# The first loads issued in stages, the experts' weights last, and new numbers in the planner of the order

## The chip, the core and the metric
The kernel runs on one NeuronCore of a Trainium2 chip. Five engines work side by side, each through its own list of instructions in its written order: TensorE (PE) multiplies, and its loads of the stationary operand are shown as PEld; VectorE (DVE); ScalarE (ACT); GpSimd (POOL); SyncE (SP), which here only starts transfers. The engines wait for each other by semaphores. Transfers between the chip's memory and the on-chip buffer (SBUF) are done by 16 DMA engines; nearly all of them are started by SP. Matrix products land in PSUM, which has 8 banks.

The metric is the time of one execution on the device in microseconds, as the median of several. The runs of the kernel before took 1142.59, 1146.7 and 1146.88 us, so the median is 1146.7 us.

## What is computed
Two layers of a Perceiver block for 64 samples of 32 tokens with width 128, everything in float32. Each layer is cross-attention to a context of 257 tokens, self-attention over the 32 tokens, and a mixture of 8 experts of which each token uses two. In outline:

```python
x = x + L0_xattn(layernorm(x), ctx, ctx, mask)   # 16 heads of 8, the mask hides keys
x = x + L0_attn(layernorm(x))                    # causal, with Pluecker lines as an added bias
x = x + L0_ffn(layernorm(x))                     # 8 experts, silu(gate) * up, best 2 of the best 2 groups
x = x + L1_xattn(layernorm(x), ctx, ctx)         # no mask
x = x + L1_attn(layernorm(x))                    # causal
x = x + L1_ffn(layernorm(x))                     # 8 experts, relu, best 2 of 8
return x
# scores of L0_xattn: s = q.k / sqrt(8);  s = s + where(mask == 0, -1e9, s);  softmax over 257 keys
```

## The kernel before
**Tiling.** Four samples make a group of 128 token rows, so there are 16 groups. They are shared out over three streams, 0, 1 and 2, each with its own set of buffers (`ctxT0`, `maskb0`, `P0` and so on). Stream 0 has six turns, streams 1 and 2 have five. The three streams are in flight together, so that PE has work from one while another waits.

**Order.** No engine's order is written by hand. `group_tasks` lists the tasks of one group with their needs: `kproj`, `vproj` and `kvtail` (keys and values from the context), `mask`, `ln`, `lnT`, `qproj`, `bq` (the queries spread out by head, `spread`), `scores`, `soft` (softmax), `ptrans` and `pv` (weights transposed, times values), `tailV`, `sel`, `rT`, `norm`, `oproj` (the end of the cross-attention, in `On` and then `xs`), then `qk`, `vself`, `lines` to `jlines`, `sscore` to `spv` (self-attention), `route` to `pick`, `up` and `down` (the experts). `list_schedule` then plays all tasks of all groups through against a duration for each, and writes down an order for PE, DVE, ACT and POOL, a PSUM bank for each result, and the order of SP's later loads. Which ready task goes first is set by a priority that holds the tables `BONUS` and `WHEN` and the constants `STICK`, `EAGER`, `REACH`, `LAG`. Two more tables tell the planner when inputs come: `FIRST` gives the earliest start of the first tasks of each stream, and `ARRIVES` the delay that it reckons for a reload in later turns (6.0 us for the mask). The tables decide only the order; on the chip each engine waits for what is really there.

**First loads.** SP starts all first loads in one go, without a wait: `bcol` and the first three weights of `wsq`, then for each stream `ctxT` (514 KB), `xin` (64 KB) and four copies of the mask (128.5 KB each), with the constants `cst` in stream 0's part and the other small weights (`wsq`, `brow`, `router`, `b2`) in stream 2's part, and right behind them the experts' weights: `w13` 2048 KB, `w2a` 1024 KB, `w1` 2048 KB, `w2b` 2048 KB. Only then come the reloads of later turns, each of which waits until its buffer is free. The first of them is the mask of stream 0 for its second turn: it waits for the last masked softmax step of stream 0 in the first turn.

**The mask.** A mask is converted on POOL (L718), reduced on DVE (L1152, L1154), and then used by DVE's masked softmax step (L1187). POOL and DVE have the conversion of stream 0's second mask in the middle of their orders, while streams 1 and 2 are still in their first turn: whatever stands behind it on these two engines waits for the transfer too.

**Lines that the prediction speaks of** (of the kernel before; those behind SP's block are 11 higher in the changed kernel): L661, L667, L673 (SP: `ctxT`, `xin`, `maskb`), L688 (SP: experts), L718, L745, L772, L782, L795 and L798, L802 (POOL: mask, `spread`, a square root of the lines, `LQ`, the sums of `norm`, the self-attention's weights), L725 (POOL: `rstd`), L878 (PE: `ptrans`), L913 (PE: `oproj`), L957 (PE: `sscore`), L991 (PE: `up`), L1230 (DVE: `xs` after `oproj`).

Of the kernel before, what the change touches and what calls it, by code (L numbers as in the profile page):

```python
# [399 lines left out]
BONUS = {("bo", 0, PE): -24.56, ("bo", 0, DVE): -172.31, ("bq", 0, POOL): 435.89, ("bq", 1, POOL): 294.24,  # L400
         ("down", 0, PE): -3.88, ("down", 0, DVE): 1140.48, ("down", 1, PE): -23.73, ("down", 1, DVE): -642.6,
         ("groups", 0, DVE): -666.24, ("jlines", 0, PE): 226.43, ("jlines", 0, VACT): -301.7,
         ("kproj", 0, PE): -82.44, ("kproj", 0, VACT): -62.34, ("kproj", 1, PE): -300.02,
         ("kproj", 1, VACT): -421.52, ("kvtail", 0, PE): 65.43, ("kvtail", 0, DVE): -32.49,
         ("kvtail", 1, PE): -706.66, ("kvtail", 1, DVE): -892.6, ("lines", 0, PE): 573.82,
         ("lines", 0, VACT): -1047.17, ("lines", 0, POOL): -14.44, ("linesN", 0, DVE): 410.16,
         ("linesN", 0, POOL): -1284.74, ("linesT", 0, PE): 27.38, ("linesT", 0, VACT): 541.34,
         ("linesT", 0, POOL): 659.68, ("linesU", 0, DVE): 840.54, ("linesU", 0, POOL): 213.22,
         ("ln", 0, DVE): -26.08, ("ln", 0, POOL): 294.5, ("ln", 1, DVE): 13.88, ("ln", 1, POOL): -759.28,
         ("lnT", 0, PE): 445.73, ("lnT", 0, DVE): 687.26, ("lnT", 0, VACT): -105.05, ("lnT", 1, PE): 89.47,  # L410
         ("lnT", 1, DVE): 330.28, ("lnT", 1, VACT): -15.37, ("mask", 0, DVE): -305.15, ("mask", 0, POOL): 38.85,
         ("norm", 0, DVE): 860.3, ("norm", 0, POOL): 92.47, ("norm", 1, DVE): 975.38, ("norm", 1, POOL): 1244.98,
         ("oproj", 0, PE): 567.81, ("oproj", 0, DVE): -251.96, ("oproj", 1, PE): 549.66, ("oproj", 1, DVE): 786.95,
         ("pick", 0, DVE): 450.3, ("pick", 1, DVE): 268.79, ("ptrans", 0, PE): -10.71, ("ptrans", 0, VACT): -29.09,
         ("ptrans", 1, PE): 155.2, ("ptrans", 1, VACT): 530.74, ("pv", 0, PE): 745.89, ("pv", 1, PE): 39.36,
         ("qk", 0, PE): 276.11, ("qk", 0, VACT): 179.08, ("qk", 0, POOL): 1160.11, ("qk", 1, PE): 551.51,
         ("qk", 1, VACT): -30.44, ("qk", 1, POOL): 1198.39, ("qproj", 0, PE): 85.23, ("qproj", 0, VACT): -628.38,
         ("qproj", 1, PE): 386.09, ("qproj", 1, VACT): -252.75, ("rT", 0, PE): -300.59, ("rT", 1, PE): 577.99,
         ("route", 0, PE): 309.97, ("route", 0, DVE): 952.83, ("route", 0, VACT): 1317.83, ("route", 1, PE): 1275.74,
         ("route", 1, DVE): 1019.06, ("route", 1, VACT): -928.27, ("scores", 0, PE): 36.22, ("scores", 1, PE): 32.03,  # L420
# [1012 lines left out]
```

## Time and profile before

| what | value |
|---|---|
| median of three runs | 1146.7 us (1142.59 to 1146.88) |
| the profiled execution's own time | 1144.7 us |
| its span | 1142.9 us |
| mean granted clock of TensorE | 0.988 of full speed |
| PE busy | 1083.9 us, 95% |
| PE weight loads busy | 908.6 us, 80% |
| DVE busy | 838.9 us, 73% |
| ACT busy | 725.8 us, 64% |
| POOL busy | 511.4 us, 45% |
| moved by DMA | 30.33 MB, of it 27.05 MB read from memory |

The span is from the first to the last instruction of one profiled execution. A busy time is the time in which an engine had an instruction in work. PE is busy in 95% of the span, so what can be won without taking work away is the remaining 59.0 us, and what is lost while PE is busy at the lower of its two clocks. The stream of the DMA is dense in the first 44 us only.

### The profile page before, as it was taken

To read this page: it belongs to the slowest core of one execution; us is meant where nothing else is said; L and a number is where in the kernel's file an instruction comes from. 1 tells how busy PE (TensorE), PEld (TensorE's weight loads), DVE (VectorE), ACT (ScalarE), POOL (GpSimd) and SP (SyncE) were. 2 spreads that over 40 slices of the span, in tenths; PEclk is the share of its full clock that TensorE was granted. 3 is DMA by queue.
4 is the path that set the end of the run, shared out by engine and by line. 5 is a ranking of instruction groups with operands and counts; after the bars stand their busy time and mean duration, and the time that the engine had idled before them with its cause. 6 is when DMAs were issued, how large, how long until landed. Compare 5 with 4: busy or idle time off the path is not lost.

```text
span 1142.9 us, 34921 instructions
## 1 busy us (share of the span) xinstructions
PE 1083.9 (95%) x13032; PEld 908.6 (80%) x13032; DVE 838.9 (73%) x2865; ACT 725.8 (64%) x2305; POOL 511.4 (45%) x712
## 2 busy tenths in 40 slices
PE   7798899999999999999999999999999999999898
PEld 5477787788877978887878878788788788887698
DVE  4455977687878866867868688686878757877785
ACT  6682478765676495667575775747657766556742
POOL 5386234435654345355444445354453354343430
PEclk9897999999999999999999999999999999999999
DMA  9520000000010000010000001010000000000000
GB/s 291 193 60 18 2 2 2 25 17 15 20 57 2 5 23 6 21 41 23 22 5 20 5 23 41 13 31 4 23 2 22 2 5 2 5 1 2 2 2 8
DMA packets 17748, 30.33 MB, mean 27 GB/s; under 512 B 2216, under 2 KB 14640, under 8 KB 16944
## 3 DMA queue, kind: packets, MB, share of 16 engines
q1 hardware_dynamic: 15280, 27.06, 7.8%
q8 instruction: 108, 1.77, 0.6%
q10 hardware_dynamic: 2304, 1.05, 0.3%
q14 instruction: 56, 0.46, 0.1%
HBM read 27.05 MB, written 1.05 MB: 25 GB/s over the span
## 4 chain that ended last, share of the span: by engine, by line
PE 61%; DVE 20%; ACT 9%; issue 5%; POOL 4%; DMA 2%; SPq 0%; DVEq 0%; ACTq 0%; POOLq 0%
PE bank L999 12%; PE bank L991 11%; PE bank L878 7%; PE bank L871 5%; PE bank L890 4%; PE bank L845 3%; PE bank L838 3%; PE bank L957 3%; ACT P L1039 3%; PE bank L976 2%; ACT PT L1050 2%; DVE P L1329 2%; DVE P L1319 2%; DMA maskb<-mask_in 2%; DVE xs L1339 2%
## 5 line engine op out<-in xcount | busy, mean ns | idle before, releaser
L991 PE MATMUL bank<-xnT,w 128*128 128x128 f32 x2048 | 259.4, 279 | 5.1 <-DVE P L1322 2.6
L991 PEld LDWEIGHTS bank<-xnT,w 128*128 128x128 f32 x2048 | 242.1, 193 | 11.7 <-issue 3.8
L1050 ACT COPY PT<-bank 128x512 f32<-128x512 f32 x256 | 149.9, 592 | 30.9 <-PE bank L878 29.1
L878 PE MATMUL bank<-cst,P 128*128 128x128 f32 x1024 | 153.8, 279 | 10.7 <-DVE nmax L1187 8.4
L878 PEld LDWEIGHTS bank<-cst,P 128*128 128x128 f32 x1024 | 114.3, 142 | 34.6 <-issue 14.5
L1042 ACT ACTIVATE P<-bank,nmax 128x257 f32<-128x257 f32 x256 | 123.2, 491 | 27.5 <-DVE nmax L1191 26.8
L1039 ACT ACTIVATE P<-P,nmax 128x257 f32<-128x257 f32 x256 | 131.7, 517 | 13.7 <-DVE nmax L1187 13.1
L999 PE MATMUL bank<-w2b,P 128*128 128x128 f32 x1024 | 130.8, 278 | 0.0
L1187 DVE CUSTOM_DVE_ANT_0 P<-bank,maskb,mscale 128x257 f32<-128x257 f32 x256 | 114.0, 481 | 20.9 <-PE bank L871 20.6
L999 PEld LDWEIGHTS bank<-w2b,P 128*128 128x128 f32 x1024 | 121.0, 192 | 5.7 <-issue 4.5
L1191 DVE TENSOR_REDUCE nmax<-bank 128x1 f32<-128x257 f32 x256 | 96.5, 413 | 39.1 <-PE bank L871 38.8
L1339 DVE SCALAR_TENSOR_TENSOR xs<-bank,comb,xs 128x128 f32<-128x128 f32 x256 | 88.2, 345 | 45.0 <-PE bank L999 39.1
L795 POOL TENSOR_TENSOR On<-On 128x256 f32<-128x256 f32 x64 | 46.8, 732 | 140.6 <-DVE On L1223 140.3
L1104 ACT ACTIVATE P<-bank,bcol 128x128 f32<-128x128 f32 x256 | 73.2, 369 | 48.8 <-PE bank L991 35.6
L871 PE MATMUL bank<-KT,spread 32*128 32x257 f32 x1024 | 92.0, 429 | 8.0 <-ACT PT L1050 1.9
L1097 ACT ACTIVATE P<-bank 128x256 f32<-128x256 f32 x128 | 49.4, 388 | 68.2 <-PE bank L991 48.0
L745 POOL TENSOR_TENSOR spread<-qs,cst 128x512 f32<-128x512 f32 x64 | 66.6, 1043 | 55.5 <-ACT qs L1033 32.2
L890 PE MATMUL bank<-PT,V 128*32 128x128 f32 x2048 | 81.9, 280 | 1.5 <-ACT PT L1050 1.5
L999 PE MATMUL bank<-w2a,P 128*128 128x128 f32 x512 | 73.3, 280 | 2.7 <-DVE P L1322 1.9
L838 PE MATMUL bank<-ctxT,wsq 128*128 128x512 f32 x128 | 68.7, 629 | 7.1 <-DMA ctxT<-ctx_in 5.7
L1329 DVE TENSOR_SCALAR P<-bank,bcol 128x128 f32<-128x128 f32 x256 | 71.2, 341 | 5.0 <-PE bank L999 3.1
L890 PEld LDWEIGHTS bank<-PT,V 128*32 128x32 f32 x2048 | 48.8, 109 | 29.1 <-ACT PT L1050 13.6
(133 smaller groups left out, 2198.4 us busy)
## 6 DMA issues: line engine op xcount, KB each, us to landing
ctxT<-ctx_in SPq DMA_DIRECT2D x16, 514.0 KB, 3.7
maskb<-mask_in SPq DMA_DIRECT2D x64, 128.5 KB, 2.8
w<-w_in SPq DMA_DIRECT2D x2, 2048.0 KB, 17.9
w2b<-w2b_in SPq DMA_DIRECT2D x1, 2048.0 KB, 26.1
wsq<-wsq_in SPq DMA_DIRECT2D x1, 1032.0 KB
xin<-x_in SPq DMA_DIRECT2D x16, 64.0 KB, 1.9
w2a<-w2a_in SPq DMA_DIRECT2D x1, 1024.0 KB, 17.2
out<-xs ACTq DMA_DIRECT2D x16, 64.0 KB, 1.5
```

The source lines that it names most:

```text
L838: nc.tensor.matmul(ps[:, :], w(f"k{l}"), ctxT[s][:, m * 512:m * 512 + 512], start=True, stop=True).then_inc(full, 1)
L871: nc.tensor.matmul(bank[bank_of[step, i, g]][:, 0:SK], BQ[s][rows, m, :, :], KT[s][rows, m, :], start=True, stop=True, tile_position=(32 * ...
L878: ins = nc.tensor.transpose(ps[:, k * 128:k * 128 + 128], P[s][:, 2 * m + k // 2, (k % 2) * 128:(k % 2) * 128 + 128], ident)
L890: ins = nc.tensor.matmul(ps[32 * g:32 * g + 32, 128 * m:128 * m + 128], V[s][:, 2 * m + k, 32 * g:32 * g + 32], PT[:, place_of[s, l, m, i] ...
L991: ins = nc.tensor.matmul(ps[:, k * 128:k * 128 + 128], wt[:, m, k * 128:k * 128 + 128], xnT[s][:, :], start=True, stop=True)
L999: ins = nc.tensor.matmul(ps[:, 0:128], HT[s][m % SLOTS][:, k * 128:k * 128 + 128], wt[:, m, k, :], start=(k == 0), stop=(k == nk - 1))
L1039: nc.scalar.activation(P[s][:, m, :], P[s][:, m, :], ACT.Exp, bias=nmax[s][:, m:m + 1], scale=-1.0, accum_out=sums[s][:, m:m + 1]).then_in ...
L1042: nc.scalar.activation(P[s][:, m, :], ps[:, 0:SK], ACT.Exp, bias=nmax[s][:, m:m + 1], accum_out=sums[s][:, m:m + 1]).then_inc(exp_done[s], 1)
L1050: nc.scalar.copy(PT[:, place, m % 2 * 512:m % 2 * 512 + 512], ps[:, :]).then_inc(pt_done[s], 1)
L1187: nc.vector.tensor_tensor_reduce(P[s][:, m, :], ps[:, 0:SK], mbias[s][:, b, :], mscale[s][:, b:b + 1], LOWEST, ALU.add, ALU.min, nmax[s][: ...
L1191: nc.vector.tensor_reduce(nmax[s][:, m:m + 1], ps[:, 0:SK], X, ALU.max, negate=True).then_inc(max_done[s], 1)
L1339: nc.vector.scalar_tensor_tensor(xs[s][:, :], ps[:, 0:128], comb[s][:, m:m + 1], xs[s][:, :], ALU.mult, ALU.add).then_inc(x_done[s], 1)
```

## The change
SP's first loads are the same transfers of the same sizes. They are now issued in stages, and SP waits between them: after `ctxT0`, `xin0` and `cst` it waits for `ctxT0` to land; then come the mask of stream 0, `ctxT1`, `xin1`; a wait for that mask; the mask of stream 1, `ctxT2`, `xin2`; a wait for `ctxT1`; the other small weights; a wait for the mask of stream 1; the mask of stream 2; a wait for the small weights; `w13` and `w2a`; a wait for these two; `w1` and `w2b`. The reloads of the second turn follow as before. The planner's `FIRST` has new numbers, and `STICK`, `EAGER`, `LAG`, `BONUS` and `WHEN` have new ones too, so the order of all four computing engines changes from the first turn to the last. Tasks, durations in the planner, tiles and instructions are the same.

```diff
@@ -100,8 +100,8 @@
-FIRST = {("kproj", PE): (4.8, 9.7, 13.6), ("ln", DVE): (5.2, 10.0, 13.9), ("xpb", POOL): (5.2, 10.0, 13.9),
-         ("mask", POOL): (7.9, 11.8, 19.5), ("bo", PE): (20.5,), ("up", PE): (30.0, 30.0, 30.0)}
+FIRST = {("kproj", PE): (5.8, 9.5, 13.0), ("ln", DVE): (5.8, 9.5, 13.0), ("xpb", POOL): (5.8, 9.5, 13.0),
+         ("mask", POOL): (9.5, 13.0, 20.0), ("bo", PE): (18.0,), ("up", PE): (32.0, 32.0, 32.0)}
@@ -395,47 +395,47 @@
-STICK = 0.421
-EAGER, REACH, LAG = 0.1333, 0.001, 32.81
-BONUS = {("bo", 0, PE): -24.56, ("bo", 0, DVE): -172.31, ("bq", 0, POOL): 435.89, ("bq", 1, POOL): 294.24,
...
+STICK = 0.690
+EAGER, REACH, LAG = 0.0412, 0.000, 30.07
+BONUS = {("bo", 0, PE): -482.13, ("bo", 0, DVE): -413.15, ("bq", 0, POOL): 535.15, ("bq", 1, POOL): 113.54,
...
@@ -673,19 +673,30 @@
-            for s in range(STREAMS):
-                load_ctx(0, s)
-                load_x(0, s)
-                if s == 0:
-                    sp.dma_start(cst[:, :], const_d).then_inc(constants_in, 16)
-                elif s == STREAMS - 1:
-                    for dst, src in ((wsq[:, WFIRST:WSQ], wsq_d[:, WFIRST:WSQ]), (rows_in, brow_d[:, 0:512]),
-                                     (router[:, :], brow_d[:, 512:520]), (b2[:, :], b2_d)):
-                        sp.dma_start(dst, src).then_inc(others_in, 16)
-                load_mask(0, s)
-            for dst, src, loaded in ((w13[:, :, :], w13_d, experts0_in), (w2a[:, :, :, :], w2a_d, experts0_in),
-                                     (w1[:, :, :], w1_d, experts1_in), (w2b[:, :, :, :], w2b_d, experts1_in)):
-                sp.dma_start(dst, src).then_inc(loaded, 16)
+            load_ctx(0, 0)
+            load_x(0, 0)
+            sp.dma_start(cst[:, :], const_d).then_inc(constants_in, 16)
+
+            sp.wait_ge(ctx_in[0], 16)
+            load_mask(0, 0)
+            load_ctx(0, 1)
+            load_x(0, 1)
+            sp.wait_ge(mask_in[0], 64)
+            load_mask(0, 1)
+            load_ctx(0, 2)
+            load_x(0, 2)
+            sp.wait_ge(ctx_in[1], 16)
+            for dst, src in ((wsq[:, WFIRST:WSQ], wsq_d[:, WFIRST:WSQ]), (rows_in, brow_d[:, 0:512]),
+                             (router[:, :], brow_d[:, 512:520]), (b2[:, :], b2_d)):
+                sp.dma_start(dst, src).then_inc(others_in, 16)
+            sp.wait_ge(mask_in[1], 64)
+            load_mask(0, 2)
+            sp.wait_ge(others_in, 16 * OTHER_LOADS)
+            for dst, src in ((w13[:, :, :], w13_d), (w2a[:, :, :, :], w2a_d)):
+                sp.dma_start(dst, src).then_inc(experts0_in, 16)
+            sp.wait_ge(experts0_in, 16 * EXPERT_LOADS)
+            for dst, src in ((w1[:, :, :], w1_d), (w2b[:, :, :, :], w2b_d)):
+                sp.dma_start(dst, src).then_inc(experts1_in, 16)
```

Two places of the new order matter below. The first is DVE around the second mask of stream 0. `mmin0` and `mscale0` are the two steps on that mask, `P1,nmax1` is one masked softmax step of stream 1, `On0` the end of stream 0's cross-attention in the first turn and `xs0` its result. Before:

```order
L1187 ISA P1,nmax1<-bank4,maskb1,mscale1 128x257
L1187 ISA nmax1 128x1
L1209 TENSOR_TENSOR On0<-bank1,On0 128x4x4x32
L1152 TENSOR_REDUCE mmin0<-maskb0 128x4
L1154 TENSOR_SCALAR mscale0<-mmin0 128x4
L1187 ISA P1,nmax1<-bank4,maskb1,mscale1 128x257
L1187 ISA nmax1 128x1
L1187 ISA P1,nmax1<-bank1,maskb1,mscale1 128x257
```

and in the changed kernel:

```order
L1220 TENSOR_TENSOR On0<-bank0,On0 128x4x4x32
L1198 ISA P1,nmax1<-bank2,maskb1,mscale1 128x257
L1198 ISA nmax1 128x1
L1234 TENSOR_TENSOR On0<-bank7,On0 128x4x4x32
L1163 TENSOR_REDUCE mmin0<-maskb0 128x4
L1165 TENSOR_SCALAR mscale0<-mmin0 128x4
L1198 ISA P1,nmax1<-bank5,maskb1,mscale1 128x257
L1198 ISA nmax1 128x1
L1198 ISA P1,nmax1<-bank6,maskb1,mscale1 128x257
L1198 ISA nmax1 128x1
L1241 TENSOR_TENSOR xs0<-bank5,xpb0 128x128
```

The second step on `On0` (L1223 before, L1234 now) stood behind the mask and behind four more softmax steps of stream 1; it now stands ahead of the mask. `xs0` (L1230 before, L1241 now) came six softmax steps and `On0` after the mask; it now comes two softmax steps after it. Ten softmax steps of stream 1 are done ahead of the mask instead of twelve.

The second place is POOL, some thirty instructions further on, in the self-attention of the first turn. `maskb2` is the conversion of stream 2's second mask, `P0<-P0,nmax0` and `P0<-P0,rsum0` are the softmax of stream 0's self-attention, and `P1<-P1,cst` is the last step that stream 1's `sscore` (PE) needs. Before:

```order
L752 TENSOR_TENSOR spread2<-rsum2,cst 128x512
L772 TENSOR_TENSOR lnn1<-lss1,cst 128x16
L789 TENSOR_TENSOR P0<-P0,nmax0 128x512
L776 TENSOR_TENSOR lp1<-P1,lrn1 128x16x6
L795 TENSOR_TENSOR On2<-On2 128x256
L798 TENSOR_TENSOR On2<-On2 128x128
L782 TENSOR_TENSOR P1<-P1,cst 128x512
L802 TENSOR_TENSOR P0<-P0,rsum0 128x512
L737 TENSOR_TENSOR xpb2<-xs2,bo 128x128
L723 TENSOR_TENSOR veps2<-mv2,cst 128x1
L725 TENSOR_TENSOR rstd2<-veps2,cst 128x1
L718 TENSOR_SCALAR maskb2<-maskb2 128x1028
```

and in the changed kernel:

```order
L763 TENSOR_TENSOR spread2<-rsum2,cst 128x512
L729 TENSOR_SCALAR maskb2<-maskb2 128x1028
L800 TENSOR_TENSOR P0<-P0,nmax0 128x512
L756 TENSOR_TENSOR spread1<-qs1,cst 128x512
L770 TENSOR_TENSOR P1<-P1 128x96
L772 TENSOR_TENSOR P1<-P1 128x96
L775 TENSOR_TENSOR P1<-P1 128x96
L778 TENSOR_TENSOR P1<-P1 128x96
L813 TENSOR_TENSOR P0<-P0,rsum0 128x512
L806 TENSOR_TENSOR On2<-On2 128x256
L809 TENSOR_TENSOR On2<-On2 128x128
L783 TENSOR_TENSOR lnn1<-lss1,cst 128x16
```

The mask of stream 2 is converted earlier, ahead of both softmax steps of stream 0, and stream 1's lines (`lnn1`, and the `P1<-P1,cst` that is not in the piece any more) come later.

## Rows read from the trace of the kernel before

**Rows 1.** The page: the span, and its part 1 (busy, share, instructions).
```profile
span 1142.9 us, 34921 instructions
PE 1083.9 (95%) x13032; PEld 908.6 (80%) x13032; DVE 838.9 (73%) x2865; ACT 725.8 (64%) x2305; POOL 511.4 (45%) x712
```

**Rows 2.** Waits, 0 to 60 us: total, times, longest.
```profile
POOL maskb L718 <- DMA maskb<-mask_in: 13.1, 3, 10.2
...
PE bank L878 <- DVE nmax L1187: 8.4, 1, 8.4
...
PE bank L838 <- DMA ctxT<-ctx_in: 5.7, 1, 5.7
```

**Rows 3.** Timeline, 28 to 62 us: start, length, engine, line, what.
```profile
29.71 1.75 SPq L673 DMA_DIRECT2D maskb<-mask_in  x4
...
40.45 0.66 PE L878 MATMUL bank<-cst,P 128*128 128x128 f32 x4
...
43.76 3.72 POOL L718 TENSOR_SCALAR maskb<-maskb 128x1028 f32<-128x1028 int32 x1 [10.21 <-DMA maskb<-mask_in]
47.51 1.23 DVE L1152 TENSOR_REDUCE mmin<-maskb 128x4 f32<-128x1028 f32 x1 [9.11 <-POOL maskb L718]
48.77 0.17 DVE L1154 TENSOR_SCALAR mscale<-mmin 128x4 f32<-128x4 f32 x1
...
49.48 1.11 PE L878 MATMUL bank<-cst,P 128*128 128x128 f32 x4 [8.38 <-DVE nmax L1187]
...
52.26 0.72 POOL L795 TENSOR_TENSOR On<-On 128x256 f32<-128x256 f32 x1 [4.78 <-DVE On L1223]
...
53.06 0.46 POOL L798 TENSOR_TENSOR On<-On 128x128 f32<-128x128 f32 x1
...
56.03 0.29 DVE L1230 TENSOR_TENSOR xs<-bank,xpb 128x128 f32<-128x128 f32 x1
...
56.39 0.46 POOL L737 TENSOR_TENSOR xpb<-xs,bo 128x128 f32<-128x128 f32 x1 [2.88 <-DVE xs L1230]
```

**Rows 4.** The chain that ended last, in order of time: start, length, what.
```profile
31.04 12.54 DMA maskb<-mask_in
```

**Rows 5.** DMA issues, windows 14.8:15.85 and 15.85:17 (w1, w2b), 0:2.5, all: us to landing.
```profile
w<-w_in SPq DMA_DIRECT2D x1, 2048.0 KB, 20.6
w2b<-w2b_in SPq DMA_DIRECT2D x1, 2048.0 KB, 26.1
ctxT<-ctx_in SPq DMA_DIRECT2D x1, 514.0 KB, 3.7
xin<-x_in SPq DMA_DIRECT2D x16, 64.0 KB, 1.9
```

**Rows 6.** Windows: busy of each engine, PE clock, DMA share, GB/s.
```profile
20.00:41.00 21.00, 20.51 (x221) 14.05 (x220) 14.18 (x56) 21.00 (x71) 9.06 (x9) 1.00 1.03 382
60.00:103.00 43.00, 36.63 (x529) 28.21 (x528) 22.52 (x75) 24.19 (x73) 36.98 (x44) 0.87 0.16 51
103.00:1143.00 1040.00, 1001.88 (x12128) 849.51 (x12127) 788.31 (x2686) 662.52 (x2118) 445.94 (x636) 1.00 0.05 14
```

**Rows 7.** Timeline of POOL, 44 to 110 us.
```profile
84.96 1.04 POOL L782 TENSOR_TENSOR P<-P,cst 128x512 f32<-128x512 f32 x1
...
88.19 3.72 POOL L718 TENSOR_SCALAR maskb<-maskb 128x1028 f32<-128x1028 int32 x1
...
98.57 0.58 POOL L725 TENSOR_TENSOR rstd<-veps,cst 128x1 f32<-128x1 f32 x1
```

**Rows 8.** Timeline of PE, 74 to 125 us.
```profile
86.21 0.42 PE L957 MATMUL bank<-qs,spread 32*128 32x32 f32 x8 [0.60 <-POOL P L782]
...
102.42 6.29 PE L991 MATMUL bank<-xnT,w 128*128 128x128 f32 x40
```

**Rows 9.** POOL by line, 60 to 103 us: busy, mean ns, idle before.
```profile
L772 POOL TENSOR_TENSOR lnn<-lss,cst 128x16 f32<-128x16 f32 x3 | 8.7, 2910 | 0.4 <-DVE lss L1233 0.4
L718 POOL TENSOR_SCALAR maskb<-maskb 128x1028 f32<-128x1028 int32 x2 | 7.4, 3718 | 0.0
L745 POOL TENSOR_TENSOR spread<-qs,cst 128x512 f32<-128x512 f32 x3 | 3.1, 1040 | 1.1 <-ACT qs L1063 1.1
```

More of the change, by code:

```diff
@@ L395, in build_order @@
     return orders, banks, place_of, [(what, g) for _, g, what in sorted(loads)]
-STICK = 0.421
-EAGER, REACH, LAG = 0.1333, 0.001, 32.81
-BONUS = {("bo", 0, PE): -24.56, ("bo", 0, DVE): -172.31, ("bq", 0, POOL): 435.89, ("bq", 1, POOL): 294.24,
[L401 to L420, printed above, removed]
-         ("sel", 0, DVE): -51.25, ("sel", 0, POOL): -190.63, ("sel", 1, DVE): 451.89, ("sel", 1, POOL): 49.03,
-         ("snorm", 0, DVE): 331.79, ("snorm", 0, POOL): 26.67, ("snorm", 1, DVE): 532.48,
-         ("snorm", 1, POOL): 1588.41, ("soft", 0, DVE): -169.19, ("soft", 0, VACT): 220.64, ("soft", 1, DVE): 775.14,
-         ("soft", 1, VACT): -113.0, ("sptrans", 0, PE): 87.4, ("sptrans", 0, VACT): 218.19,
-         ("sptrans", 1, PE): 31.73, ("sptrans", 1, VACT): -698.98, ("spv", 0, PE): 969.93, ("spv", 1, PE): -28.24,
-         ("sscore", 0, PE): 37.09, ("sscore", 0, DVE): -730.27, ("sscore", 0, VACT): -1262.05,
-         ("sscore", 0, POOL): 965.95, ("sscore", 1, PE): 1247.23, ("sscore", 1, DVE): -1642.22,
-         ("sscore", 1, VACT): 237.96, ("sscore", 1, POOL): -1512.73, ("store", 1, VACT): -167.63,
-         ("tailV", 0, PE): 404.74, ("tailV", 0, DVE): -1192.1, ("tailV", 0, VACT): -452.37,
-         ("tailV", 0, POOL): 554.98, ("tailV", 1, PE): 519.3, ("tailV", 1, DVE): 380.92, ("tailV", 1, VACT): 48.48,
-         ("tailV", 1, POOL): 309.42, ("up", 0, PE): -4.36, ("up", 0, DVE): -146.21, ("up", 0, VACT): -61.36,
-         ("up", 1, PE): -19.92, ("up", 1, DVE): 829.73, ("up", 1, VACT): 290.54, ("vproj", 0, PE): -346.28,
-         ("vproj", 0, VACT): 206.78, ("vproj", 1, PE): -152.56, ("vproj", 1, VACT): -95.05, ("vself", 0, PE): 29.27,
-         ("vself", 0, VACT): 291.57, ("vself", 1, PE): -125.12, ("vself", 1, VACT): -506.54, ("wT", 1, PE): -59.3,
-         ("wT", 1, VACT): 342.9, ("wb2", 1, PE): 456.33, ("wb2", 1, DVE): 65.4, ("xpb", 0, POOL): 396.57,
-         ("xpb", 1, POOL): -843.62}
@@ L441 @@
+WHEN = [85.41, -39.92, -28.9, 23.32, 19.49, 3.23, -11.29, 31.51,
+        8.49, -16.2, -1.04, -15.51, 95.66, -35.96, 91.8, 265.22]
 WCOL = {}
```

38 lines of the change are left out of this document (36 added, 2 removed).

## The prediction
> **What bounds the kernel now.** First the page's part 1: PE is busy in 1083.9 of 1142.9 us [rows 1], so 59.0 us are left that an order or an earlier load could win. Then the waits of the first 60 us: PE sits 5.7 us until the first context is there, and 8.4 us in one piece for a DVE step [rows 2]. The timeline shows what is behind that piece. SP starts the mask of stream 0's second turn at 29.71, the conversion on POOL starts at 43.76, DVE reduces it from 47.51, and PE goes on at 49.48 after its last transposes of 40.45 [rows 3]. The mask takes that long because it stands in the queue behind the experts: `w2b`, started at 15.89, lands 26.1 us later, at 42.0 [rows 5], and the last of the mask's four copies at 31.04 + 12.54 = 43.6 [rows 4]. The experts themselves are not needed before PE's first `up` at 102.42 [rows 8]. Third, the windows: between 20 and 41 us PE is busy 20.51 of 21.00 and ACT 21.00 of 21.00, so there no load is missing. Between 60 and 103 us POOL is busy 36.98 of 43.00, PE is idle 6.4, and the granted clock is 0.87, which is the lower level (1.2 instead of 2.4 GHz) for 26% of the stretch and so 0.13 x 43 = 5.6 us lost; it falls after PE's gaps for POOL. In the 1040 us that follow PE is idle 38.1 us in small pieces [rows 6]. So there are four places: the start, the wait for the mask, the POOL-bound stretch, and the long rest.
>
> **The change, the loads.** No byte is taken away. The first context is started as before and lands 3.7 us later, so the first 5.7 us stay. SP's waits add dry spells of the queue where nothing else is in flight. A small transfer alone takes 1.9 us from start to landing [rows 5]; of 64 KB at the 382 GB/s of the dense stretch [rows 6] that is 0.2 us of data, so about 1.7 us are dry when a stage waits for everything ahead of it. That is fully so once, between `w2a` and `w1`: +1.7. At the first wait `xin0` and `cst` (330 KB, 0.9 us) are still in flight: +0.8. At the other four waits a context or a mask (0.5 MB, 1.4 us or more) is behind the one waited for: about 0. The sum is 2.5; with `ctxT0` already under way I take +2.4. The four first reloads still come behind `w1` and `w2b` in SP's order, and the rows show that the queue is worked off in order, so the mask lands at 43.6 + 2.4 = 46.0. From below, the order of small and large transfers could make the queue a little better: -1. From above, all six waits dry: 6 x 1.9 = +11.4. I stay near the lower rows, since four of six waits have cover.
>
> The Trainium skill, DMA: Bandwidth & Descriptors, section "Anatomy of one DMA", states a fixed part of about 2.0 us per DMA on the path from GpSimd, most of it the receipt after the last byte, and a term of bytes over 436 GB/s. That speaks against stages: two dry spells would be 4.0 us by it instead of 2.4, and the sum below would end at 1145.3 instead of 1143.7. The rows of the small transfers, at 1.9 us, nearly agree with its fixed part; whether a stage pays all of it no row of this trace shows.
>
> **The wait for the mask.** Before, PE went on 5.9 us after the landing (49.48 - 43.6): conversion, two DVE steps, one softmax step. Now `On0` is complete on DVE ahead of the mask, so POOL adds it up right behind the conversion: 0.2 + 3.72 + 0.72 + 0.46 [rows 3], and PE's `oproj` follows, about 5.1 us after the landing, at 51.1. PE has about the same work ahead of the wait as before (eight halves of keys, seven of values, 32 score matrices, twelve transposes), and `rT` (0.6 us) in addition. So PE resumes 1.6 us later than at 49.5, with 0.6 us more done: +1.0 by itself. The conversion of mask 0 is what POOL and DVE both wait for, so nothing else fills it.
>
> **Stream 0's lead.** The waits of POOL behind the conversion shrink. The 4.78 us for `On` go entirely [rows 3]. The 2.88 us for `xs` shrink to about 1.7: POOL ends its sums 5.1 us after the landing, and `xs0` comes on DVE after 3.9 + 1.23 + 0.17 and two softmax steps of 0.48, near 6.4, and ends at 6.7; saved 1.2. I add up POOL's instructions from this conversion to stream 0's third `rstd` (18 groups of POOL by line; the three costliest in [rows 9], with 2.91, 3.72 and 1.04 us each): 42.8 us before, 42.3 us now, 0.5 less. Before, that `rstd` ended at 98.57 + 0.58 = 99.15 [rows 7]. Now: 99.15 + 2.4 - 0.5 - 4.8 - 1.2 = 95.05, 4.1 us earlier. I give back 1.1 for a new wait of the size of the one for `spread` [rows 9], and take -3.0. PE's `up` of stream 0 hangs on it, 3.3 us later before (102.42). The PE work ahead of that `up` is the same, so what comes earlier is PE idle time that goes, and everything behind moves up by it. The +2.4 and the +1.0 are inside this -3.0. The bounds: if the whole POOL-bound hole closes, 6.4 of idle and 5.6 of clock go, -12.0; if nothing of the lead arrives, the landing stays, +2.4.
>
> **The long rest.** The order after 103 us is another one with the same instructions. The trace cannot show it. From 38.1 us of idle a quarter either way is 9.5 us; the nearest row is the stretch as it is, so I take 0 and keep 6 either way for the range.
>
> **Sum.** -3.0 on the profiled execution: 1144.7 - 3.0 = 1141.7. That execution is 2.0 below the median of the runs, so for a median 1146.7 - 3.0 = 1143.7.
>
> **The rivals.**
> 1. The hole closes. For it: the idle time there comes in pieces of 0.5 to 2.6 us behind POOL, and stream 0 has the missing work 4 us earlier; if PE has no gap long enough, the clock stays at its upper level. Against it: POOL's work there is not less. Worked out: three quarters of 12.0, so -9.0, 1137.7.
> 2. Slower: stream 1 starves. POOL's work from the conversion to the `P1<-P1,cst` that PE's `sscore` of stream 1 needs grows from 31.7 to 38.9 us: the conversion of mask 2 (3.72), `On0` (1.2), `rstd2` (0.8), `xpb2` (0.5) and `P0<-P0,rsum0` (1.05) now stand ahead. PE has that `sscore` ahead of stream 0's `up`. Before it started at 86.21 behind the POOL step of 84.96 [rows 7, 8]; with the shorter waits it would start at 46.2 + 38.9 + 4.5 = 89.6 plus 0.2, which is covered. If POOL's waits don't shrink it starts near 96, and it decides once it starts after 99.1 (102.4 less 2.0 for its own 64 products and 1.3 to `up`). Price: 7.2 + 2.4 less 1.2 = +8.4, 1155.1. Against it: the lead of 4.8 us rests on one clear line of DVE's order.
> 3. The loads are hidden and the change does nothing: ACT and PE are full between 20 and 41 us [rows 6], the experts are needed at 102, the late landing eats stream 0's lead. Then it is the order alone, and 1146.7.
>
> **How the numbers follow.** The forecast, -3.0 with its own range 1140 to 1147: 0.36. Rival 1: 0.29. Rival 2, with the like of it later in the program: 0.21. Rival 3: 0.14. About 0.5%, 5.7 us, is what a measurement of this kernel can tell from no change. Faster by more than that: rival 1 (0.27 of its 0.29) and the lower edge of the forecast (0.09), 0.36. Slower: rival 2 (0.19) and the upper edges of the others (0.02), 0.21. Within: 0.43. For 8 in 10 the range goes from 1137.7 less 5.7 for the long rest, 1132, to rival 2's 1155.
>
> **What would show it.** Right, if in the changed kernel the conversion of stream 0's second mask starts at 45 to 47.5 us; if the rate of the DMA shows one gap of about 1.7 us near 30 us and none of this size later; if POOL's first sum of `On0` follows the conversion without a wait; if `up` of stream 0 starts between 96 and 100 us; and if PE is idle in the window to 103 us by 2 to 4 us less. Wrong in its first step, if the mask lands before 44 or after 49. Wrong in the second, if `sscore` of stream 1 starts after 94. Wrong in the last, if the idle time of PE after 103 us is off 38 by more than 6; then the time was made by the new order of the long rest, and not by the loads.

## The result and the profile after

The changed kernel is slower. Its median is 1164.32 us (four runs, 1162.94 to 1166.84) against 1145.91 for the kernel before (four runs, 1142.59 to 1146.88): ratio 1.0171, 95% interval 1.0151 to 1.0191. The forecast was 1143.7, with a range from 1132 to 1155.

The page's span and part 1 of the changed kernel:

```profile
span 1161.2 us, 34921 instructions
PE 1094.6 (94%) x13032; PEld 920.9 (79%) x13032; DVE 844.8 (73%) x2865; ACT 723.1 (62%) x2305; POOL 510.9 (44%) x712
```

Against [rows 1] the span grew by 18.3 us. The count of PE's instructions is the same, 13032, and so is the work in them, but PE is busy 10.7 us longer (1094.6 - 1083.9) and idle 7.6 us longer (66.6 - 59.0). The clock explains it: the mean granted clock fell from 0.988 to 0.973. Before, PE was busy at the lower level for 20.4 us (in 44.3 to 54.5, 88.7 to 95.5, 98.9 to 105.7 and 1034.2 to 1037.6), in the changed kernel for 45.9 us. At half the speed that costs 10.2 and 22.9 us. Taken off the busy time, it leaves 1073.7 and 1071.6 us, the same work within some 2 us. So only two fifths of the loss are waits, and three fifths are the lower of the two clock levels.

The waits of the changed kernel: PE from 0 to 110 us (four rows), POOL from 0 to 110 us (one), PE from 103 to 150 us (the last):

```profile
PE bank L924 <- DVE nmax L1198: 12.1, 1, 12.1
PE bank L849 <- DMA ctxT<-ctx_in: 7.5, 2, 5.8
PE bank L868 <- DVE xn L1187: 4.0, 3, 2.0
PE bank L976 <- POOL P L813: 2.3, 1, 2.3
...
POOL maskb L729 <- DMA maskb<-mask_in: 17.1, 3, 13.8
...
PE bank L868 <- DVE xn L1187: 6.4, 3, 3.4
```

The wait for the mask grew from 8.4 to 12.1 us on PE and from 10.2 to 13.8 on POOL [rows 2]. New is that PE waits 1.7 us for its second context (7.5 less 5.8). And after 60 us it waits longer at L868 (`lnT`, the transpose of a layernorm's result) for DVE, up to 3.4 us in one piece, where the longest was 1.8 before.

SP's timeline of the changed kernel, 20 to 70 us:

```profile
22.69 0.35 SPq L696 DMA_DIRECT2D w<-w_in  x1
23.08 1.30 SPq L696 DMA_DIRECT2D w2a<-w2a_in  x1
33.61 0.33 SPq L699 DMA_DIRECT2D w<-w_in  x1
...
34.59 1.44 SPq L667 DMA_DIRECT2D xin<-x_in  x3
36.15 25.96 SPq L673 DMA_DIRECT2D maskb<-mask_in  x8
```

and two rows of its chain of waits (start, length, what):

```profile
23.08 10.51 DMA w2a<-w2a_in
...
37.63 12.49 DMA maskb<-mask_in
```

`w13` starts at 22.69, `w1` only when `w2a` has landed at 33.6, and the mask lands at 37.63 + 12.49 = 50.1, where it was 43.6 [rows 4]. The planner orders SP's reloads too, so these did not stay as they were: the new order puts three `xin` (64 KB each) ahead of the mask, the old one has the mask first. The queue's dry places are in the windows of one microsecond (last number: GB/s):

```profile
22.00:23.00 1.00, 1.00 (x14) 0.72 (x7) 0.62 (x5) 1.00 (x5) 0.16 (x1) 1.00 0.23 61
32.00:33.00 1.00, 1.00 (x12) 0.57 (x11) 0.00 (x0) 1.00 (x4) 0.00 (x0) 1.00 0.16 66
33.00:34.00 1.00, 1.00 (x20) 0.76 (x20) 0.66 (x3) 1.00 (x4) 0.00 (x0) 1.00 0.00 0
34.00:35.00 1.00, 1.00 (x18) 0.80 (x11) 1.00 (x7) 1.00 (x4) 0.08 (x1) 1.00 1.05 197
```

What follows the mask, in the timeline of all engines:

```profile
50.31 3.72 POOL L729 TENSOR_SCALAR maskb<-maskb 128x1028 f32<-128x1028 int32 x1 [13.78 <-DMA maskb<-mask_in]
53.99 0.72 POOL L806 TENSOR_TENSOR On<-On 128x256 f32<-128x256 f32 x1
...
54.80 0.46 POOL L809 TENSOR_TENSOR On<-On 128x128 f32<-128x128 f32 x1
...
56.03 0.80 PE L924 MATMUL bank<-wsq,On 128*128 128x128 f32 x2 [12.13 <-DVE nmax L1198]
...
57.23 0.46 POOL L748 TENSOR_TENSOR xpb<-xs,bo 128x128 f32<-128x128 f32 x1 [1.98 <-DVE xs L1241]
...
63.12 0.61 POOL L819 COPY tails<-P 128x512 f32<-128x512 f32 x1 [4.12 <-ACT P L1050]
```

The sums of `On` follow the conversion without a wait, as the order said. But a new wait of 4.12 us on POOL, for ACT, comes 5 us later. ACT is then at work on softmax steps that stood behind the mask: of stream 1 only ten steps are done ahead of it, where it was twelve. PE's `sscore` of stream 1 and `up` of stream 0, which answer to [rows 8]:

```profile
103.30 0.65 PE L968 MATMUL bank<-qs,spread 32*128 32x32 f32 x8
...
108.93 0.45 PE L868 MATMUL bank<-cst,xn 128*128 128x128 f32 x1 [2.00 <-DVE xn L1187]
...
110.24 9.56 PE L1002 MATMUL bank<-xnT,w 128*128 128x128 f32 x64
...
131.49 0.30 PE L868 MATMUL bank<-cst,xn 128*128 128x128 f32 x1 [3.42 <-DVE xn L1187]
```

`sscore` is 17 us later (86.21 before), `up` 7.8 us later (102.42). The eight small products of one `sscore` row take 0.65 us where they took 0.42, since the clock is at its lower level there. What lies between them is in the timelines of POOL (first row) and DVE (the others):

```profile
104.42 0.54 POOL L736 TENSOR_TENSOR rstd<-veps,cst 128x1 f32<-128x1 f32 x1
...
106.92 0.88 DVE L1257 TENSOR_TENSOR P<-bank,cst 128x128 f32<-128x128 f32 x4 [3.44 <-PE bank L968]
107.84 0.69 DVE L1267 TENSOR_REDUCE nmax<-P 128x16 f32<-128x512 f32 x1
108.44 0.34 DVE L1187 TENSOR_SCALAR xn<-xs,mv,rstd 128x128 f32<-128x128 f32 x1
```

Stream 0's `rstd` is ready at 105.0, but its `xn` starts at 108.44 only: on DVE it stands behind the steps on the scores of stream 1, and these wait 3.44 us for PE's `sscore`. So the late `sscore` holds `up` back through DVE.

The windows that answer to [rows 6], first of the changed kernel, then of before for the one stretch not shown yet (busy times, clock, DMA share, GB/s):

```profile
60.00:103.00 43.00, 38.00 (x468) 28.19 (x470) 20.39 (x72) 28.21 (x86) 32.99 (x40) 0.86 0.22 63
103.00:150.00 47.00, 40.13 (x450) 36.76 (x442) 34.01 (x113) 13.85 (x40) 15.75 (x22) 0.80 0.01 2
103.00:1161.00 1058.00, 1017.46 (x12253) 865.61 (x12244) 798.41 (x2698) 661.38 (x2122) 451.35 (x642) 0.98 0.05 14
```

```profile
103.00:150.00 47.00, 43.18 (x450) 39.62 (x449) 42.16 (x145) 21.38 (x65) 11.88 (x20) 0.97 0.01 2
```

From 103 to 150 us the clock is 0.80 where it was 0.97. The lower level costs time only while PE works: that was for 15.3 us there (103.0 to 114.8 and 131.9 to 138.7), before for 2.7 us (103.0 to 105.7), so the difference is 6.3 us. Behind 150 us it was for 16.1 us, in four stretches (at 630.2, 828.2, 1046.7 and 1087.6), before for 3.4 us (at 1034.2): another 6.3 us. In the whole rest behind 103 us PE is idle 40.5 us (1058.0 - 1017.46), hardly more than the 38.1 before: the rest lost by clock, not by waits. A good milestone is the first output store (first row before, second row after):

```profile
210.99 0.37 ACTq L1110 DMA_DIRECT2D out<-xs  x1
```

```profile
225.56 0.38 ACTq L1121 DMA_DIRECT2D out<-xs  x1
```

It is 14.6 us later, and the last store 18.2. Four fifths of the loss are made ahead of the first output store.

### The profile page after: what moved, and what is told of

Its sections match the earlier page's. It is cut to its first block, busy times and chain, and to the rows that moved or that the text cites. A ratio compares the mean times of both kernels' runs of the same rounds, so it can differ in the third digit from the quotient of the medians.

```text
span 1161.2 us, 34921 instructions
## 1 busy us (share of the span) xinstructions
PE 1094.6 (94%) x13032; PEld 920.9 (79%) x13032; DVE 844.8 (73%) x2865; ACT 723.1 (62%) x2305; POOL 510.9 (44%) x712
## 4 chain that ended last, share of the span: by engine, by line
PE 65%; DVE 16%; ACT 9%; issue 4%; DMA 3%; POOL 2%; SPq 1%; DVEq 0%; ACTq 0%; POOLq 0%
PE bank L1002 14%; PE bank L1010 13%; PE bank L889 7%; PE bank L882 5%; PE bank L901 4%; PE bank L856 4%; PE bank L968 3%; ACT P L1050 3%; PE bank L849 3%; PE bank L987 2%; ACT PT L1061 2%; DVE P L1330 1%; DVE xs L1350 1%; PE bank L924 1%; DMA maskb<-mask_in 1%
## 5 line engine op out<-in xcount | busy, mean ns | idle before, releaser
L1002 PE MATMUL bank<-xnT,w 128*128 128x128 f32 x2048 | 263.2, 281 | 4.2 <-DVE P L1333 2.8
L1002 PEld LDWEIGHTS bank<-xnT,w 128*128 128x128 f32 x2048 | 245.5, 195 | 11.8 <-issue 5.0
L889 PE MATMUL bank<-cst,P 128*128 128x128 f32 x1024 | 156.6, 282 | 1.2 <-ACT P L1053 0.6
L889 PEld LDWEIGHTS bank<-cst,P 128*128 128x128 f32 x1024 | 117.6, 144 | 27.0 <-issue 16.4
L1010 PEld LDWEIGHTS bank<-w2a,P 128*128 128x128 f32 x512 | 64.8, 194 | 13.1 <-issue 4.1
```

Of the source, the lines that this page charges most:

```text
L889: ins = nc.tensor.transpose(ps[:, k * 128:k * 128 + 128], P[s][:, 2 * m + k // 2, (k % 2) * 128:(k % 2) * 128 + 128], ident)
L1002: ins = nc.tensor.matmul(ps[:, k * 128:k * 128 + 128], wt[:, m, k * 128:k * 128 + 128], xnT[s][:, :], start=True, stop=True)
L1010: ins = nc.tensor.matmul(ps[:, 0:128], HT[s][m % SLOTS][:, k * 128:k * 128 + 128], wt[:, m, k, :], start=(k == 0), stop=(k == nk - 1))
```

## The experiments

Twelve kernels, each timed beside the kernel before on the same chip. Eight of them have two axes, so they are best read in one table; e7 to e10 come below. "New order" are the changed planner tables and `FIRST`; the conversion is that of stream 0's second mask on POOL, which starts when the mask has landed (in the two kernels of 36.83 and 33.50 it has landed before); the difference is between medians of the same session.

| order | loads | conversion at us | against before, us | ratio |
|---|---|---|---|---|
| old | e3: reloads ahead of `w1`, `w2b` | 33.50 | -9.2 | 0.9912 |
| old | e11: stages, reloads ahead | 37.35 | -6.1 | 0.9941 |
| old | before | 43.76 | 0 | 1 |
| old | e5: stages, last two waits left out | 46.64 | +2.3 | 1.003 |
| old | e6: the last two waits alone | 47.76 | +2.6 | 1.0031 |
| old | e2: stages | 49.42 | +5.6 | 1.0043 |
| new | e12: old loads, reloads ahead | 36.83 | +4.9 | 1.0053 |
| new | e4: stages, reloads ahead | 38.67 | +3.5 | 1.0034 |
| new | e1: old loads | 43.33 | +12.1 | 1.01 |
| new | the changed kernel | 50.31 | +18.4 | 1.0171 |

Down each half the time follows the mask, but for e4, which is 1.4 us faster than e12 with a conversion 1.8 us later (their intervals overlap): from e3 to e2 14.8 us of time for 15.9 us of conversion, from e12 to the changed kernel 13.5 for 13.5. Between the halves, at about the same conversion, lie 12 us (e1 against before), 11 (e12 against e11), 10 (e4 against e11) and 13 (the changed kernel against e2).

**e1, the new order with the old loads.** The changed tables are put on SP's old block.

```diff
-STICK = 0.421
-EAGER, REACH, LAG = 0.1333, 0.001, 32.81
+STICK = 0.690
+EAGER, REACH, LAG = 0.0412, 0.000, 30.07
...
```

> The new planner numbers (and so the new order of all engines) with SP's old first loads, all issued at once. Theory A, the stages' dry spells cost the time (the mask of the second turn landed at 50.2 instead of 43.6 us, and what follows comes from that): the mask lands at 43 to 45 us again and the time is within 4 us of the kernel before, 1142 to 1150. Theory B, the new order by itself costs most of the 18.4 us: at least 8 us slower than before, 1154 to 1160, with TensorE at its lower clock between 100 and 140 us.

Measured: 1159.06 us against 1146.98, ratio 1.01, interval 1.0065 to 1.0135: theory B. The mean clock was 0.973 to 0.976 in its four runs and 0.979 to 0.988 in the 19 of before. PE's longest wait for the mask is 6.6 us, less than the 8.4 before, yet the kernel is 12 us slower. Its profiled execution has a span of 1156.0 us with PE busy 1096.7, so idle 59.3: +0.3 of idle, +12.8 of busy. In this execution the order alone costs clock and hardly any idle time. Here, with the mask at its old time, `up` of stream 0 starts at 101.39: 1.0 us earlier than before, where my sum had 5.4 (3.0 and the 2.4 of the later mask). The row and the window of e1:

```profile
43.33 3.72 POOL L718 TENSOR_SCALAR maskb<-maskb 128x1028 f32<-128x1028 int32 x1 [8.27 <-DMA maskb<-mask_in]
...
122.99 0.30 PE L857 MATMUL bank<-cst,xn 128*128 128x128 f32 x1 [3.42 <-DVE xn L1176]
```

```profile
60.00:150.00 90.00, 78.04 (x883) 66.54 (x881) 60.23 (x204) 41.14 (x127) 46.19 (x63) 0.85 0.09 25
```

The kernel before has 79.81 us busy and a clock of 0.92 in this window.

**e2, the old order with the stages.** SP's block of the changed kernel on the tables of before; the edit is the last part of the diff of the change.

```diff
+            sp.wait_ge(ctx_in[0], 16)
+            load_mask(0, 0)
...
+            sp.wait_ge(experts0_in, 16 * EXPERT_LOADS)
```

> The old planner numbers and the old order, with SP's first loads issued in the new stages. Theory A, the stages cost the time: the mask of the second turn lands at 48 to 51 us and the kernel is 12 to 18 us slower than before, 1158 to 1164. Theory B, the order costs most: the loads alone cost what the mask lands later, 6 to 7 us, and the time is 1151 to 1154.

Measured: 1152.62 us, ratio 1.0043, interval 1.0028 to 1.0059: theory B again. Ratio by ratio e1 (11.5 us) and e2 (4.9) make 16.4 of the change's 19.6; the intervals of the three are wide enough for the rest. PE's wait at the transposes is 13.0 us instead of 8.4:

```profile
49.42 3.72 POOL L729 TENSOR_SCALAR maskb<-maskb 128x1028 f32<-128x1028 int32 x1 [14.84 <-DMA maskb<-mask_in]
...
55.14 1.12 PE L889 MATMUL bank<-cst,P 128*128 128x128 f32 x4 [13.00 <-DVE nmax L1198]
```

**e3, the kernel before with the first reloads ahead of the second half of the experts.** SP's own waits for those four reloads stay; `w1` and `w2b` come behind them. This is the direct test of what the mask stands behind.

```diff
+            for dst, src in ((w13[:, :, :], w13_d), (w2a[:, :, :, :], w2a_d)):
+                sp.dma_start(dst, src).then_inc(experts0_in, 16)
+            for what, g in loads[:4]:
+                reload(what, g)
+            for dst, src in ((w1[:, :, :], w1_d), (w2b[:, :, :, :], w2b_d)):
+                sp.dma_start(dst, src).then_inc(experts1_in, 16)
+            for what, g in loads[4:]:
+                reload(what, g)
```

> The kernel before, with its first four reloads (the mask of stream 0's second turn and three xin) issued between the first and the second half of the experts' weights. If TensorE's wait of 8.4 us near 45 us is the queue behind the experts' weights, the mask lands at 32 to 34 us, the wait goes, the clock doesn't fall there, and the time is 8 to 12 us less, 1134 to 1138. If the POOL-bound stretch that follows (60 to 103 us) simply takes the time back, it is within 3 us of before.

Measured: 1137.83 us, ratio 0.9912, interval 0.989 to 0.9933, as expected: the best kernel of the study, faster than both. The conversion starts at 33.50, PE works through the hole, and `up` of stream 0 starts at 91.29 instead of 102.42. The window of the hole, first of e3, then of before:

```profile
41.00:60.00 19.00, 18.27 (x220) 13.43 (x218) 12.21 (x49) 17.75 (x57) 14.27 (x19) 1.00 0.32 110
```

```profile
41.00:60.00 19.00, 10.62 (x83) 7.29 (x83) 6.94 (x24) 9.27 (x29) 7.95 (x9) 0.73 0.18 42
```

7.65 us of idle time are won there, and 2.5 us of clock: before, PE was busy for 5.0 of the 10.2 us at the lower level (44.3 to 54.5). Of these 10.2 us 9.2 arrive at the end.

**e4, the same edit on the changed kernel.** Diff as for e3.

```diff
+            for what, g in loads[:4]:
+                reload(what, g)
             sp.wait_ge(experts0_in, 16 * EXPERT_LOADS)
```

> The changed kernel, with the first four reloads issued ahead of SP's wait for the first half of the experts' weights, so ahead of the second half. Theory A, the late mask is the cause of the loss: it lands near 36 us, TensorE's wait of 12.1 us goes, and the time falls by 14 to 20 us to 1144 to 1150. Theory B, the order: it falls by no more than the 12 us of the wait, to 1152 to 1156, and TensorE still runs at its lower clock between 100 and 120 us.

Measured: 1150.43 us, ratio 1.0034, interval 1.0011 to 1.0056. By the table that is 14.9 us less than the changed kernel for a conversion 11.6 us earlier (13.9 by the medians); in the old order it is 11.7 us (13.8 by the medians) for 12.1 (e11 against e2). Neither theory is right in full: the gain is more than the wait of 12.1, as theory A has it, and PE still runs at the lower level behind it, as theory B has it (79.4 to 99.9 and 117.0 to 123.8). And even with the mask 5 us earlier than before, the new order doesn't reach before. Late in this kernel, on PE:

```profile
1075.45 0.72 PE L883 MATMUL bank<-KT,spread 32*128 32x257 f32 x8 [1.29 <-POOL spread L757]
1077.26 1.46 PE L883 MATMUL bank<-KT,spread 32*128 32x257 f32 x8 [1.09 <-DVE On L1235]
```

```profile
1074.00:1077.00 3.00, 0.88 (x10) 0.34 (x8) 2.93 (x5) 0.13 (x1) 1.45 (x2) 0.85 0.00 0
1077.00:1082.00 5.00, 4.46 (x22) 3.64 (x22) 4.37 (x15) 3.86 (x13) 3.98 (x7) 0.50 0.00 0
```

PE was busy 0.88 of 3 us, and the next 5 us are at the lower level. Its clock in the window of 60 to 150 us is 0.85, as in e1, with the mask far earlier.

**e5 and e6, which of the waits cost.** e5 is e2 without the last two waits (before `w13` and before `w1`); e6 is the kernel before with those two alone.

```diff
-            sp.wait_ge(others_in, 16 * OTHER_LOADS)
...
-            sp.wait_ge(experts0_in, 16 * EXPERT_LOADS)
```

> The old order with the new stages, but without SP's last two waits (for the other small weights and for the first half of the experts' weights); the four early waits stay. Theory A, the two last waits make the queue run dry (near 22 and near 33 us) and cost the stages' 5 to 6 us: the second turn's mask lands at 43.5 to 45.5 us and the time is 1146 to 1149, within 2 us of before. Theory B, the early waits matter as much: the mask lands at 46 to 48 and the time stays above 1150.

Measured: 1149.03 us, ratio 1.003, interval 1.0014 to 1.0046. The mask lands at 33.95 + 12.50 = 46.45, as theory B has it: the four early waits cost 2.9 us of landing. The time, 2.3 us more than before, is nearer to theory A.

```profile
33.95 12.50 DMA maskb<-mask_in
```

```diff
+            sp.wait_ge(others_in, 16 * OTHER_LOADS)
             for dst, src in ((w13[:, :, :], w13_d), (w2a[:, :, :, :], w2a_d)):
                 sp.dma_start(dst, src).then_inc(experts0_in, 16)
+            sp.wait_ge(experts0_in, 16 * EXPERT_LOADS)
```

> The kernel before with only these two waits put in: for the small weights ahead of w13 and w2a, and for these two ahead of w1 and w2b. Theory A: the mask lands at 48 to 50 us instead of 43.6, and the time is 4 to 6 us more than before, 1151 to 1153. Theory B: at most 2 us more.

Measured: 1149.42 us, ratio 1.0031, interval 1.0016 to 1.0045. The mask lands at 33.75 + 13.83 = 47.6, 4.0 later, and the time is 2.6 us more than before: both lie between the two theories. So both groups of waits cost: 2.9 and 4.0 alone, 5.7 together in e2 (by the conversion). I had counted 0.8 and 1.7.

```profile
33.75 13.83 DMA maskb<-mask_in
```

**e7 and e8, does the clock come back if PE is kept at work?** Four products that nobody reads are added at nine places of the first turn, 36 in each kernel (72 rows of the trace), on e4 and on e3.

```diff
+                if (i, l) == (0, 0) and (kind == "sptrans" or kind == "lnT" and m):
+                    for _ in range(4):
+                        nc.tensor.matmul(ps[:, 0:128], w("k0"), w("v0"), start=True, stop=True)
```

> The kernel with the new order and the reloads ahead of the second half of the experts (median 1150.4), with four products of 128x128 that nobody reads ahead of each lnT (after the first) and each sptrans of layer 0 in the first turn, 9 places and about 8 us of added work. Theory C, the lower clock between 80 and 130 us costs more than the gaps themselves: the granted clock of 60 to 150 us rises from 0.84 to over 0.93 and the time falls by 2 to 6 us. Theory D, the gaps count and the clock only goes with them: the time rises by 2 to 8 us.

Measured: 1151.17 us, ratio 1.0053, interval 1.0026 to 1.0079: +0.7 against e4, within what the runs scatter. Neither theory's time came. In the profile the clock of 60 to 150 us rose from 0.85 to 0.91 and the mean from 0.977 to 0.985. Busy is 1097.1, of which the filler is an estimated 7.9 (72 rows of 0.11 us); the kernel's own work took 1089.2 instead of e4's 1095.1, so some 5.9 us of clock came back, and 1.8 of idle went. The 7.9 us were paid for it. So in this order a part of the lower clock hangs on PE's short gaps; filling them at these nine places won that part back, but no time.

```profile
60.00:150.00 90.00, 81.56 (x944) 71.37 (x944) 61.13 (x209) 38.97 (x118) 43.63 (x58) 0.91 0.09 25
```

> The kernel with the old order and the reloads ahead of the second half of the experts (median 1137.8), with the same filler products in the same 9 places. Theory C: the clock of 60 to 150 us rises from 0.92 to over 0.97, and the time falls by 1 to 4 us. Theory D: it rises by 2 to 8 us.

Measured: 1139.75 us, ratio 0.9938, interval 0.9921 to 0.9954, +1.9 against e3. The clock of that window stayed 0.92, and PE's idle time fell from 50.5 to 46.1 us. There the filler found waits to fill, and in the window no clock to win back (the mean went from 0.988 to 0.991).

**e9 and e10, which of the new numbers.** e9 is the kernel before with the new `FIRST`, e10 with the new `STICK`, `EAGER`, `REACH`, `LAG`, `BONUS` and `WHEN`.

```diff
-FIRST = {("kproj", PE): (4.8, 9.7, 13.6), ("ln", DVE): (5.2, 10.0, 13.9), ("xpb", POOL): (5.2, 10.0, 13.9),
-         ("mask", POOL): (7.9, 11.8, 19.5), ("bo", PE): (20.5,), ("up", PE): (30.0, 30.0, 30.0)}
+FIRST = {("kproj", PE): (5.8, 9.5, 13.0), ("ln", DVE): (5.8, 9.5, 13.0), ("xpb", POOL): (5.8, 9.5, 13.0),
+         ("mask", POOL): (9.5, 13.0, 20.0), ("bo", PE): (18.0,), ("up", PE): (32.0, 32.0, 32.0)}
```

> The kernel before with only the table FIRST changed; the loads and the priorities are the old ones, and the order differs in part. Theory E, the new arrival times are what made the order worse: 6 to 12 us slower than before, with TensorE's busy time up by 8 or more. Theory F, the searched priorities did: within 4 us of before, and busy within 3 us of 1083.9.

Measured: 1154.54 us, ratio 1.0077, interval 1.0054 to 1.0101. The time is theory E's; PE's busy time is not, 1088.3, so 4.4 us up.

```diff
-STICK = 0.421
+STICK = 0.690
...
```

> The kernel before with only the priorities changed (STICK, EAGER, REACH, LAG, BONUS, WHEN); the loads and FIRST are the old ones. Theory E: within 4 us of before. Theory F, the searched priorities give an order that starves TensorE more often for a microsecond or two, whatever the arrival times: 8 to 14 us slower than before, with TensorE's busy time at 1092 or more and a mean clock of 0.978 or less.

Measured: 1177.71 us, ratio 1.0289, interval 1.0249 to 1.033; PE busy 1105.1 and idle 70.5 of 1175.6, clock 0.966. That is theory F's direction, at more than twice its size. The new tables with the old `FIRST` are worse than both together (e1, +12.1), and `FIRST` shifted by a few us under the old tables costs 7.8. So the loss can't be shared out between them: the three other orders drawn from the same planner, with the old loads, were worse by 8, 12 and 31 us. Nor is the new set the better one for the new loads: with the stages the new order is 13 us behind the old one (the changed kernel against e2).

**e11 and e12, both axes with an early mask.** e11 is e2 and e12 is e1, each with e3's edit.

```diff
+            for what, g in loads[:4]:
+                reload(what, g)
...
```

> The old order, the new stages, and the first four reloads ahead of the second half of the experts' weights. Theory A, the stages cost only by making the second turn's mask late: with the mask out of the way the time is that of the same kernel without stages (1137.8), within 3 us. Rival: the stages also delay the second stream's context and masks, which costs by itself; then it is 1141 to 1146.

Measured: 1138.8 us, ratio 0.9941, interval 0.992 to 0.9962: theory A. With the reloads ahead of `w1` the stages cost 1 to 3 us against e3 (by medians, and by the differences in the table), for a conversion 3.9 us later: no more than the later mask explains.

> The new order with the old loads and the first four reloads ahead of the second half of the experts' weights. The new order's cost does not come from the late mask: 1147 to 1152, 10 to 13 us above the same loads with the old order (1137.8), nearly all of it in TensorE's busy time (1095 against 1084.7). Rival, the new order only suffers from late loads: 1138 to 1142.

Measured: 1149.8 us, ratio 1.0053, interval 1.0033 to 1.0072, as expected and not the rival. Against e11, of the same session, that is 11 us. Against e3, its twin in the old order, it is 12 by the medians (14 by the table), about as between e1 and before; the span differs by 11.6 us, of which PE's busy time makes 8.5 (1093.2 against 1084.7). Its worst wait stands in the same place with the same length as in e1 and in the changed kernel:

```profile
113.97 0.45 PE L859 MATMUL bank<-cst,xn 128*128 128x128 f32 x1 [3.42 <-DVE xn L1178]
```

## Why the prediction was wrong

**The loads: right in kind, mis-sized.** I had 2.4 us for the dry spells, and the mask landed 6.5 later (43.6 to 50.1). The stages alone make 5.7 of it (e2, by the conversion: 43.76 to 49.42). Where the 0.9 on top (50.31) come from isn't shown. The three `xin` now ahead of the mask, which I had not counted, are an estimated 0.5 us at 382 GB/s, but e1, with the same list and the old loads, converts 0.4 us earlier than before. "Fully so once, between `w2a` and `w1`: +1.7" was too little: the rates of 66, 0 and 197 GB/s at 32 to 35 us are, against the 382 of the dense stretch, 2.3 us lost. "At the other four waits ... about 0" was the failed part. I took 0.5 MB of cover as enough; e5 shows 2.9 us for the early four. The rate at 22 us is down to 61 GB/s, where SP waits for the small weights with one mask behind them. The last two waits alone make 4.0 in e6. And "the first 5.7 us stay" holds, but the second context now comes late too, and PE waits 1.7 us for it.

I had weighed a rule of the Trainium skill (DMA: Bandwidth & Descriptors, section "Anatomy of one DMA"), a fixed part of about 2.0 us for each DMA, stated there for the path from GpSimd. By it two dry spells are an estimated 4.0 us; the trace agrees, since e6, which has just the last two waits, puts the mask 4.0 us later. The rule was nearer than my 2.4, and still short of the 6.5, because the early waits aren't free.

**The wait for the mask: right.** 5.1 us from landing to PE's `oproj` were forecast, 5.9 measured (50.1 to 56.03); POOL's sums follow the conversion without a wait, as forecast.

**Stream 0's lead: the step that failed first.** The 4.78 us on POOL did go, and the wait for `xs` is 1.98, near the 1.7 forecast. But the lead was not kept. A new wait of 4.12 us on POOL, for ACT (`tails`), took the place of the 4.78 at once; I had given back 1.1 for a new wait. e1, with the same order and the old loads, has this wait too, 3.62 us. From the conversion to stream 0's third `rstd` POOL waited 12.9 us before. By my sum 8.0 were to be left (less 4.8 and 1.2, plus 1.1), and it was 12.6. POOL's own work there is 0.5 us less, as forecast. `up` was to be at 99.4 (102.42 - 3.0) and is at 110.24. Of these 10.8 us, 4.1 are the landing (6.5 less 2.4) and 6.7 the lead: 4.7 up to the `rstd`, and 2.0 from there to `up` (5.3 us instead of 3.3), where `xn` stands behind stream 1's scores on DVE. e1 says it without the stages: 1.0 us earlier, where 5.4 were due.

**Rival 2's mechanism came true.** Its condition was that POOL's waits don't shrink, and they did not. `sscore` of stream 1 starts at 103.3, past the 99.1 from which I said it decides; it ends at 106.9, and `up` follows through DVE, as shown above. I gave it 0.21 since I trusted the shorter waits of POOL. Its price, +8.4, is near the +7.8 of `up`; it is the later part that it lacked.

**The long rest: idle right, busy wrong.** 38 us of idle ± 6 were forecast, 40.5 measured. The time still grew, by 6.8 us from `up` to the first store and by 3.7 from there to the end (10.8 + 6.8 + 3.7 = 21.3, the whole miss in the span). The step that failed is "so I take 0": I had priced the order of the rest by idle time alone, and the clock only for the hole between 60 and 103 us. That it would cost more behind 103 us stood nowhere in the sum, and it is 6.3 us up to 150 and 6.3 behind. My sign for a late loss, idle time off 38 by more than 6, could not see it. (The 5.6 us of clock in the hole were too much as well: 0.13 x 43 counts idle time too, and PE was busy at the lower level for 9 us of it, so 4.6.) The worst single gap is the `lnT` of the wait of 3.42 us. It has the same length in the changed kernel, e1, e4 and e12, with the mask at four different times, so it belongs to the order. In the windows of the changed kernel around it PE is at the lower level for the 6 us behind the gap:

```profile
128.00:130.00 2.00, 0.07 (x1) 0.00 (x0) 1.71 (x8) 0.46 (x1) 1.54 (x3) 1.00 0.00 0
...
132.00:134.00 2.00, 1.27 (x6) 1.30 (x7) 0.79 (x3) 0.63 (x3) 0.50 (x1) 0.50 0.00 0
134.00:136.00 2.00, 2.00 (x12) 2.00 (x11) 1.31 (x8) 0.59 (x2) 0.00 (x0) 0.50 0.00 0
136.00:138.00 2.00, 2.00 (x11) 2.00 (x9) 1.90 (x6) 0.75 (x2) 1.04 (x1) 0.50 0.00 0
```

Not every fall of the clock stands behind a gap. In the changed kernel it fell at 84.1 us after 3.5 us in which PE was never idle, but worked on the small products of `sscore` for about half of the time; the windows ahead of the fall and behind it are:

```profile
80.60:84.10 3.50, 3.50 (x86) 3.29 (x88) 1.05 (x7) 1.64 (x5) 3.42 (x6) 1.00 0.77 196
84.10:87.50 3.40, 3.40 (x29) 3.01 (x22) 1.64 (x6) 1.41 (x5) 3.40 (x2) 0.50 0.32 125
```

e1 has the same at 76.0. Before, at the `sscore` of 76.77, the clock stayed up. What makes the difference no run here shows.

**The cause in one line.** Of the +18.4 us, some 12 are the new order (e1; e12 against e3), most of it PE's work done at the lower clock, and about 5 to 6 are the stages (e2), by the mask that they make late. Open is which entries of the tables leave the new gaps: e9 and e10 show only that the numbers don't act one by one. That the gaps are what lowers the clock is shown in part only (e7), and the falls behind 150 us, half of the added cost of the clock behind 103 us, were not tested: filler for the late gaps wasn't tried.

## What to carry to other kernels

A small reload that is needed soon belongs ahead of a bulk load that is needed late: moving four reloads past 4 MB of weights won 9 us here, while waits between the loads only moved everything behind them back. New tables of the planner are a change of their own: run the new order alone and the new loads alone before the two together. When an order is judged, take idle time and busy time apart; here the work was equal, the rise in busy time was the clock, and it was the larger part.
